# Thirty filler products fewer on TensorE between the fourth scores and the first expert unit

## The reference, cut to what matters

```python
x = x + L0_attn(layernorm(x))     # ternary weights, rows rounded to 8 bits, 16 heads of 8, causal
x = x + L0_xattn(ctx, layernorm(x))  # cross attention over the context, with a mask
x = x + L0_ffn(layernorm(x))      # 8 experts, 2 chosen per token, 128 -> 512 -> 128, silu gate
x = x + L1_attn(layernorm(x))     # linear attention: cumulative sums of k v
x = x + L1_xattn(layernorm(x), ctx)  # picks for each token the most similar context row
x = x + L1_ffn(layernorm(x))      # 128 -> 512 -> 128, piecewise-linear gelu, 8-bit fractions
```

## Time and profile before

| | us |
|---|---|
| median of 3 runs | 340.92 |
| lowest, highest | 340.58, 344.45 |
| the profiled execution's own time | 341.06 |
| its span, first to last instruction | 339.3 |
| TensorE products busy | 286.5 (84%) |
| VectorE busy | 234.2 (69%) |
| ScalarE busy | 187.8 (55%) |
| GpSimd busy | 158.0 (47%) |
| chain that ended last, TensorE's share | 60% |
| the same, VectorE / ScalarE / unexplained issue | 12% / 9% / 8% |

### The profile page before, as it was taken

One profiled execution on the slowest core, in us unless ns is written; L12 is line 12 of the kernel. 1 busy time (PEld: TensorE's weight loads), 2 busy tenths in 40 slices (PEclk: granted clock), 3 DMA queues, 4 the chain that ended last, 5 costly groups with the idle time before them and its releaser, 6 DMA issues.

```text
span 339.3 us, 11216 instructions
## 1 busy us (share of the span) xinstructions
PE 286.5 (84%) x4188; PEld 222.8 (66%) x4188; DVE 234.2 (69%) x770; ACT 187.8 (55%) x531; POOL 158.0 (47%) x235
## 2 busy tenths in 40 slices
PE   1977999999999899999899789999895489986454
PEld 0323667668766478889888679999794267853243
DVE  4866878898886685655655357655666898665784
ACT  1499754556633345545454458765475687714571
POOL 6676652429615525326684685614643843203100
PEclk9999999999999999999999999999999769999779
DMA  8990022000001112556887857445640100000001
GB/s 265 405 394 3 4 93 107 3 2 4 6 2 42 36 31 100 184 207 205 275 263 246 311 173 233 129 122 185 211 125 26 44 18 17 20 3 0 0 0 33
DMA packets 19765, 38.40 MB, mean 113 GB/s; under 512 B 2152, under 2 KB 13032, under 8 KB 19584
## 3 DMA queue, kind: packets, MB, share of 16 engines
q1 hardware_dynamic: 17504, 34.59, 30.2%
q0 software_dynamic: 1024, 2.10, 2.0%
q10 hardware_dynamic: 1184, 1.00, 0.9%
HBM read 29.88 MB, written 7.73 MB: 111 GB/s over the span
## 4 chain that ended last, share of the span: by engine, by line
PE 60%; DVE 12%; ACT 9%; issue 8%; POOL 6%; DMA 4%; POOLq 0%; ACTq 0%; DVEq 0%
PE FU L588 11%; PE OA L781 7%; PE OA L597 6%; PE FU L722 5%; PE Sp L707 4%; ACT keyT L1021 3%; PE OA L810 2%; DMA consts<-in_consts 2%; DMA keyT<-yg,home 2%; POOL keyT L507 2%; POOL rstd L468 2%; PE Sp L722 2%; PE Mp L750 2%; PE OA L821 1%; PE FU L906 1%
## 5 line engine op out<-in xcount | busy, mean ns | idle before, releaser
L588 PE MATMUL FU<-xgT,wbuf 128*128 128x128 f32 x480 | 61.7, 277 | 2.4 <-ACT xgT L926 1.1
L474 POOL TENSOR_TENSOR hh<-hh,uu 128x256 f32<-128x256 f32 x60 | 43.2, 732 | 43.6 <-DVE hh L1510 43.4
L588 PEld LDWEIGHTS FU<-xgT,wbuf 128*128 128x128 f32 x480 | 57.3, 192 | 4.0 <-DMA wbuf<-in_w 1.8
L1510 DVE SCALAR_TENSOR_TENSOR hh<-th,FU 128x256 f32<-128x256 f32 x60 | 24.4, 418 | 31.7 <-ACT uu L926 27.7
L936 ACT ACTIVATE th<-FU 128x256 f32<-128x256 f32 x60 | 23.2, 387 | 24.1 <-PE FU L588 22.4
L468 POOL TENSOR_TENSOR rms<-rms,minus_half 128x20 f32<-128x20 f32 x8 | 29.3, 3659 | 14.0 <-DVE rms L1257 14.0
L464 POOL TENSOR_SCALAR powed<-mv 128x1 f32<-128x1 f32 (+1 forms) x36 | 8.1, 226 | 57.3 <-DVE mv L1159 56.9
L597 PE MATMUL OA<-wbuf,hh 128*128 128x128 f32 x240 | 32.8, 280 | 1.3 <-POOL hh L474 1.3
L597 PEld LDWEIGHTS OA<-wbuf,hh 128*128 128x128 f32 x240 | 29.3, 191 | 2.7 <-ACT ys L926 1.2
L1034 ACT ACTIVATE pT<-FU 128x1024 f32<-128x1024 f32 x16 | 16.4, 1023 | 14.8 <-PE FU L722 14.8
L468 POOL TENSOR_TENSOR rstd<-powed,minus_half 128x1 f32<-128x1 f32 (+1 forms) x36 | 23.0, 640 | 3.0
(11 more groups left out here) (275 smaller groups left out, 686.9 us busy)
## 6 DMA issues: line engine op xcount, KB each, us to landing
wbuf<-in_w SPq DMA_DIRECT2D x30, 768.0 KB, 5.0
xg<-zeros SPq DMA_DIRECT2D x2, 2048.0 KB, 15.4
xg<-xg SPq DMA_DIRECT2D x30, 64.0 KB, 1.9
yg<-ys SPq DMA_DIRECT2D x30, 64.0 KB, 4.1
params<-in_params SPq DMA_DIRECT2D x1, 1503.5 KB, 10.2
x<-in_x ACTq DMA_DIRECT2D x1, 512.0 KB, 4.6
text<-in_ctx SPq DMA_DIRECT2D x1, 512.0 KB, 7.0
out<-x SPq DMA_DIRECT2D x4, 128.0 KB, 1.9
```

The source lines that it names most:

```text
L474: nc.gpsimd.tensor_tensor(hh[:, u % NB, :], hh[:, u % NB, :], uu[:, u % NB, :], ALU.mult)\
L588: ins = mm(FU[:, v % 2, 256 * part + P * i:256 * part + P * i + P], wbuf[:, u % WB, c:c + P], xgT[:, u % 2, :], start=True, stop=True)
L1510: v.scalar_tensor_tensor(hh[:, u % NB, :], th[:, u % NB, :], 1.0, FU[:, u % 2, 0:256], ALU.add, ALU.mult)\
```

## The change

Thirty filler words are taken out of TensorE's queue, all between `scores:3` and `gu:0`. Seven stand in the first three lines (48 to 67 us in the profile), 23 in the others (98 to 122 us). The fillers ahead of that stretch and behind it stay. No other word moves, and the other four queues are as they were.

```diff
--- before.py
+++ after.py
@@ -118,15 +118,15 @@
         fillFU0 text:0 fillFU0 text:1 fillFU0 fillAC xT:0 fillFU0 xT:1 fillOp text:2 fillQp text:3 fillSp fillFU1 xT:2 proj:0
         tk:0 xT:3 fillSp fillFU1 tk:1 fillSp proj:1 proj:2 fillOp turn:0 tk:2 tk:3 xT:4 scores:0 proj:3 fillOp turn:1 fillSp
         maxT:0 fillSp fillOp fillSp scores:1 tv:0 turn:2 again:0 scores:2 maxT:1 turn:3 values:0 proj:4 again:1 maxT:2
-        scores:3 swap:0 values:1 again:2 maxT:3 swap:1 fillOp fillSp fillFU1 yT:0 tv:1 yT:1 turn:4 out:0 tv:2 again:3 tnT:0
-        out:1 values:2 tv:3 fillFU0 values:3 swap:2 scores:4 xT:5 yT:2 xT:6 proj:5 out:2 swap:3 scores:5 yT:3 tnT:1 out:3
-        maxT:4 fillFU1 fillQp proj:6 maxT:5 again:4 xT:7 fillQp scores:6 proj:7 xT:8 values:4 xT:9 proj:8 proj:9 scores:7
+        scores:3 swap:0 values:1 again:2 maxT:3 swap:1 yT:0 tv:1 yT:1 turn:4 out:0 tv:2 again:3 tnT:0
+        out:1 values:2 tv:3 values:3 swap:2 scores:4 xT:5 yT:2 xT:6 proj:5 out:2 swap:3 scores:5 yT:3 tnT:1 out:3
+        maxT:4 proj:6 maxT:5 again:4 xT:7 scores:6 proj:7 xT:8 values:4 xT:9 proj:8 proj:9 scores:7
         xT:10 proj:10 again:5 maxT:6 scores:8 maxT:7 again:6 swap:4 values:5 tnT:2 again:7 maxT:8 yT:4 values:6 turn:9 out:4
         tnT:3 again:8 xT:11 yT:5 values:7 proj:11 out:5 scores:9 yT:6 turn:10 out:6 values:8 yT:7 maxT:9 scores:10 yT:8 xT:12
-        turn:11 out:7 again:9 maxT:10 pT:0 out:8 scores:11 logits:0 proj:12 again:10 fillMp scores:12 rank:0 values:9 maxT:11
-        fillAC fillFU0 fillAC fillFU0 pT:1 maxT:12 fillQp logits:1 again:11 values:10 rank:1 again:12 fillOp swap:9 values:11
-        fillFU1 fillAC swap:10 fillFU0 yT:9 fillQp out:9 fillMp fillSp yT:10 fillMp fillQp fillMp xT:13 fillSp fillAC out:10
-        proj:13 swap:11 fillOp scores:13 fillAC values:12 yT:11 maxT:13 fillFU0 fillFU0 out:11 again:13 fillSp xgT:0 yT:12
+        turn:11 out:7 again:9 maxT:10 pT:0 out:8 scores:11 logits:0 proj:12 again:10 scores:12 rank:0 values:9 maxT:11
+        pT:1 maxT:12 logits:1 again:11 values:10 rank:1 again:12 swap:9 values:11
+        swap:10 yT:9 out:9 yT:10 xT:13 out:10
+        proj:13 swap:11 scores:13 values:12 yT:11 maxT:13 out:11 again:13 xgT:0 yT:12
         xT:14 gu:0 proj:14 gu:1 xT:15 values:13 xgT:1 scores:14 xgT:2 yT:13 gu:2 gu:3 maxT:14 down:0 xgT:3 gu:4 gu:5 down:1
         proj:15 xgT:4 again:14 out:12 scores:15 out:13 gu:6 gu:7 xgT:5 down:2 gu:8 gu:9 values:14 xgT:6 gu:10 maxT:15 yT:14
         pT:2 gu:11 down:3 logits:2 down:4 xgT:7 again:15 down:5 rank:2 gu:12 values:15 out:14 gu:13 xgT:8 yT:15 gu:14 out:15
```

## The result

| | before | after |
|---|---|---|
| median of 5 runs, us | 340.84 | 348.07 |
| lowest, highest | 340.53, 344.45 | 345.64, 348.31 |
| the profiled execution's own time | 341.06 | 345.64 |
| its span | 339.3 | 343.7 |
| mean granted clock over it | 0.968 | 0.926 |

The ratio is 1.017 (1.012 to 1.022). I had forecast 340.6 us, at most 343.6. The execution that was profiled is the fastest of the five, 4.6 us over that of before; the other four had a lower mean clock, 0.906 to 0.916, so the trace shows 4.6 of the 7.2 us that the medians differ by.

What follows compares the result with a forecast made beforehand. TensorE looked full from 98 to 123 us, partly with fillers, so what stands behind each filler decides. 341.06 - 1.8 (gain) + 1.5 (clock) = 340.8, set against the 0.14 us lower median: 340.6 us; range 338.3 to 343.6.

Steps and rivals of the forecast that it cites:

- Part 1: Seven fillers between 48 and 67 us: taking them out gains 0.2 us, bounds 0 and 1.6.
- yT:0: At 49.09 us, three fillers ahead of it: 0.1 us won, since it then waits for ScalarE's pieces.
- Part 2: 23 fillers between 98 and 122 us, walked wait by wait: gain 1.6 us, bounds 0.6 and 5.1.
- maxT:12: At 102.24 us: five fillers ahead give 0.31 us, limited by VectorE's maximum ending at 101.87 us.
- yT:9: At 111.31 us, three fillers ahead: 1.23 us sooner in all, out:9 and the update of x moving with it.
- GpSimd as the limit: Behind out:9, GpSimd's rstd must follow a scatter ending at 112.33 us at best, so xT:13 gains 1.15 us.
- GpSimd's rstd directly behind the scatter: Sign of being right: ahead of xT:13, rstd starts as soon as the scatter ends.
- TensorE's wait ahead of xT:13: Sign of being right: TensorE idles some 1.5 us there once the fillers are gone.
- Part 3: The clock falls once between 112 and 116 us: a loss of 1.5 us, bounds 0 and 3.4.
- rival C: Clock low from about 113 us until the first expert unit, costing 3.4 us: 342.5 us, chance 0.2.
- the 0.45 that I had behind xT:13: Gain behind xT:13: two fillers give 0.05 us, the one ahead of values:12 some 0.4 us.
- rival B: The clock holds throughout: gain of 1.8 us and no loss, 339.1 us, chance 0.25.

Runs made afterwards that it cites:

- after_b: The changed kernel (all 30 fillers out) run again unchanged, against the kernel before on the same chip: 346.77 us, ratio 1.019.
- keep3: Against the kernel before, 24 of the 30 fillers out; only the six between yT:9 and xT:13 stay: 345.97 us, ratio 1.014.
- early7: Against the kernel before, only the seven fillers between 48 and 67 us out: 351.0 us, ratio 1.001.
- lift8: All 30 fillers out, eight others put in as one burst ahead of scores:13; against the kernel before 355.45 us, ratio 1.011.
- waits6_d: Against the kernel before, only the six fillers between yT:9 and xT:13 out: 343.15 us, ratio 1.008.
- L4: Group of seven fillers behind xT:13; taken out alone against the kernel before: 349.12 us, ratio 0.997.
- L1: Group of six fillers from scores:12 to logits:1; taken out alone against the kernel before, in the repeat: 351.98 us, ratio 1.005.
- L3: Group of six fillers between yT:9 and xT:13; taken out alone against the kernel before, in the clearest run: 343.15 us, ratio 1.008.
- L2: Group of four fillers from swap:9 to yT:9; not run alone.

## Why the prediction was wrong

**Part 1, the early seven: right in size, wrong in what I held against it.** I said 0.2 us, measured was 0.32, though not where I had it: 0.03 at yT:0, where I said 0.1, and the rest between 71 and 76 us, behind the last three fillers. I didn't ask what the three fillers ahead of yT:0 do for the clock. In after_b, keep3 and early7 it falls near 49.5 us and takes 1.3 us or more back; in the kernel after it didn't.

**Part 2, the walk: most steps failed, for two reasons, a bank and a fall of the clock at 102.5 us.**
- maxT:12 gained 0.02 us, not 0.31. I looked at its input only. It writes bank Mp, which VectorE's addition for job 11 still reads; in the kernel after it starts once that addition is over. The trace of the kernel before had shown the same, 0.05 us ahead of maxT:12 at 102.24 us:

```profile
101.78 0.41 DVE L1336 TENSOR_TENSOR qT<-qT,Mp 128x256 f32<-128x256 f32 x1
```

Timeline of the kernel after, with a third line for the next point:

```profile
100.92 0.41 DVE L1336 TENSOR_TENSOR qT<-qT,Mp 128x256 f32<-128x256 f32 x1
...
101.39 0.44 PE L750 MATMUL Mp<-consts,mpad 128*128 128x128 f32 x2 [0.83 <-DVE qT L1336]
...
111.75 0.35 DVE L1385 SCALAR_TENSOR_TENSOR x<-OA,oscale,x 128x128 f32<-128x128 f32 x1 [0.72 <-POOL oscale L523]
```

- yT:9 came 0.46 us sooner against swap:9, near the 0.60 of my working. But the last line above shows that the update of x didn't follow it: it waited for GpSimd's oscale. I had named GpSimd as the limit, one step too late.
- GpSimd's rstd directly behind the scatter was right, and so was TensorE's wait ahead of xT:13 in kind: 2.04 us, where I said 1.5. Three rows of GpSimd in the same timeline:

```profile
108.91 0.96 POOL L496 DMA_INDIRECT xg<-xall,slot  x1 [3.68 <-DVE slot L1436]
...
112.17 0.98 POOL L496 DMA_INDIRECT xg<-xall,slot  x1 [0.54 <-issue]
...
113.19 0.26 POOL L464 TENSOR_SCALAR powed<-mv 128x1 f32<-128x1 f32 x1
```

The scatter was late itself, 112.17 us where I had 111.63 - 0.31 = 111.32: the first fall of the clock stretched again:11 (1.16 to 1.99 us), rank:1 stands behind that, and the slots for the scatters came 0.55 us later than before. All four scatters up to 105 us had been 0.85 us early, so the first fall cost GpSimd's queue 1.4 us, and oscale and rstd stand in that queue. That fall lies where I had taken five fillers out of a stretch that I then didn't look at: TensorE is left with 2.65 of 4 us, and there it is never idle for more than 0.83 us at a time.

**Part 3, the clock: the step that failed.** The term of +1.5 us was one fall of 3.4 us; the first fall, at 102.5 us, stood in no term at all and cost 1.4 us, and the second cost 5.0. I had written "the clock falls once, between 112 and 116 us", for 3.4 us, and "that stretch of the new kernel has few waits left". The place was right, 112.7 us. It stayed low for 17.1 us, five times as long, and in after_b for 27.3. I had the longer stretch of the tail in my own rows as evidence for rival C, and argued it away by "dense products from scores:13 on". TensorE is busy with those, small ones for the most part, for 3.5 us and more in 4, and the clock doesn't rise. In lift8 it rose behind eight wide ones. In waits6_d, which has L4, it rose after 6.8 us.

**Rival C had the mechanism and was too cheap.** I gave it 3.4 us of loss, three groups that double. Measured from xn for xT:13 to the maximum over scores:14, behind unit 0, are 5.0 us (+0.58 to +5.60). By the table: 1.65 up to the maximum over scores:13, 0.86 up to the addition ahead of again:13, 2.51 from there on; in the last, again:13 has 0.83 and the unit's first half 0.85. I stopped C's price at the first unit's door, and that is doubled too. And C kept all of the gain, while the first fall of the clock took most of it away ahead of the second.

**The sum.** My forecast was -0.2 for part 1, -1.6 for part 2 and +1.5 for the clock, -0.3 us in all. Measured is VectorE's shift at the end, +4.46 us: -0.52 at the start, -0.32 by the early seven, +0.58 up to xT:13, +5.02 from there to the maximum over scores:14, and -0.30 behind. 3.5 us of my error lie in the length of the second low stretch (5.02 against 1.5), and 2.2 us in the gain that didn't come (0.58 against -1.6). Of these 2.2, by the rows above, 1.4 are the first fall and 0.3 the bank; the 0.45 that I had behind xT:13 can't be seen in a stretch where everything came later.

Three smaller slips: the clock row has four slices below nine tenths in two places, not two slices; 112.61 - 0.31 is 112.30, not 112.33; and seven fillers at 0.22 us are 1.5, not 1.6. None changes the sum.

The Trainium skill's rule on long idle gaps ("Why this matters for your kernels" in TensorE: Matmul & The Clock Gate), which stood beside rival B, wasn't enough here. It warns of long idle times between bursts of products in the middle of a kernel; the trace shows that their absence doesn't keep the clock: the longest idle time ahead of the first fall (98 to 102.5 us) is 0.83 us, and the second comes at 112.7 us, 0.1 us into the gap of 2.04 us, behind one of 0.87. Another section of the same page, "A second HAM failure mode: psum-queue depth-cycling", tells of a kernel with bf16 products of 512 columns that cycles through PSUM's banks, where frequent short idles between groups of products make the clock swing between its two levels. That is the nearer one, and it speaks against this change; I didn't weigh it. The trace agrees in part: the idles ahead of both falls are short, but the clock stays low for 17 and 27 us of mostly busy TensorE rather than swing.

**Open.** The medians of after and after_b are 7.2 and 6.3 us over before, the trace that I explained only 4.6. The other four executions of after have a lower mean clock, but no trace. No trace of the kernel before exists on a chip of 348 to 350 us, so that the stops in again:11 also happen there is likely and not shown; neither is their cause. That it has more low clock there is shown by its executions' mean granted clock, with medians of 0.936 to 0.945 on those chips and 0.955 and 0.960 on two of 340 us; where the low clock lies is not. Whether the kernel needs all of L1 to L4, or mainly L3 and L2, is open too.

## What to carry to other kernels

A filler beside a wait can cost nothing and still be of use: here the time grew by 0.8% when six such were gone, of which the clock explains 1.9 of 3.0 us. Before you take one out, ask what work is left to TensorE there, and which products behind it would double; price a low clock up to the end of the small products, not over one short stretch. Then judge the fall of a clock by what is on the path: 10 us more of low clock in the tail cost nothing, 17 us among dependent small products cost 5.

## What the runs showed of the hardware that I had not expected

- Groups of small products take 1.7 to 1.8 times as long at the low level: 64 products of 64 x 64 1.16 and 1.99 us, 16 of 64 x 256 1.09 and 1.99, 32 of 128 x 18 1.11 and 1.90. So none of them is bounded by a latency that is the same at both levels.
- TensorE busy all the time doesn't raise the clock by itself: 4.00 of 4 us and 0.50 (after_b, 108 to 112 us).
- The same kernel takes 340 us on some chips and 348 to 350 on others, and in the traces of changed kernels on the latter TensorE's queue stops for 0.2 to 0.5 us, once to three times, inside again:11, a group of products with no wait that the profile shows.
